# A graph layer's step loop: four selection matrices in place of two, and late coefficients kept in memory

## What is computed

```python
# graph layer; feat = layernorm(x), R = 16 relations, B = 8 bases
w_full = jnp.einsum('rb,bdo->rdo', w_comp, weight)
x_rel  = jnp.einsum('nd,rdo->rno', feat, w_full)
msg    = x_rel[etypes, src] * norm                    # one row of 256 per edge
agg    = jax.ops.segment_sum(msg, dst, num_segments=N)
x      = x + relu(agg + h_bias + feat @ loop_weight)
# then: x = x + moe(layernorm(x)), the two best of 16 experts for each node
```

## Time and profile before

| | us |
|---|---|
| runs, median (lowest to highest) | 3831.26 (3829.78 to 3837.68) |
| the profiled execution | 3843.4 |
| its span, first to last instruction | 3841.7 |
| PE busy | 2433.4 |
| POOL busy | 1874.2 |
| DVE busy | 942.2 |
| ACT busy | 682.4 |

### The profile page before, as it was taken

The page is one execution under the profiler, slowest core; times in us unless marked ns, Lnnn a source line. Parts: engine busy times, 40 slices in busy tenths (PEclk is TensorE's granted clock), DMA queues, the critical chain, the costliest instruction groups (busy, mean ns, idle before and its releaser), DMA issues. The chain is left out here.

```text
span 3841.7 us, 44188 instructions
## 1 busy us (share of the span) xinstructions
PE 2433.4 (63%) x11555; PEld 1907.4 (50%) x11556; DVE 942.2 (25%) x2185; ACT 682.4 (18%) x1839; POOL 1874.2 (49%) x2177
## 2 busy tenths in 40 slices
PE   3544454554655655666666666767767756999976
PEld 1422332433543443454454455555556536888865
DVE  4611111121102112121111111112112246333336
ACT  0510000000011111111111122212222211222234
POOL 0466666566546546555545445345544201444433
PEclk9866676776877877888878877888788878999998
DMA  3442333233223223222222223222222242112135
GB/s 117 146 135 85 88 92 88 75 92 97 73 75 90 78 74 94 77 82 80 78 76 78 78 76 90 66 68 78 83 83 64 52 144 93 63 63 63 61 123 189
DMA packets 144937, 337.27 MB, mean 88 GB/s; under 512 B 36515, under 2 KB 52163, under 8 KB 144740
## 3 DMA queue, kind: packets, MB, share of 16 engines
q0 software_dynamic: 89392, 245.59, 21.9%
q1 hardware_dynamic: 34239, 51.42, 3.9%
q10 hardware_dynamic: 21252, 39.56, 3.0%
HBM read 289.22 MB, written 50.42 MB: 88 GB/s over the span
## 5 line engine op out<-in xcount | busy, mean ns | idle before, releaser
L1176 PE MATMUL psW<-rows,S 128*128 x3920 | 1192.7, 459 | 878.2 <-issue 590.9
L994 POOL DMA_INDIRECT rows<-feat,idx x1568 | 1489.9, 950 | 479.6 <-issue 460.5
L1176 PEld LDWEIGHTS psW<-rows,S 128*128 128x128 f32 x3920 | 850.2, 228 | 1215.1 <-issue 1095.4
L1076 DVE TENSOR_TENSOR S<-psHere,coefS 128x896 f32<-128x896 f32 x280 | 303.8, 1091 | 2227.8 <-PE psW L1176 1244.3
L1235 ACT COPY z<-psW 128x256 f32<-128x256 f32 x392 | 145.6, 371 | 2064.1 <-PE psW L1176 1080.2
L977 POOL COPY idx<-srcT 128x7 int32 (+1 forms) x224 | 43.6, 195 | 783.9 <-PE psW L1176 616.4
L1139 PE MATMUL psG<-wb,zT 128*128 128x256 f32 (+1 forms) x1600 | 357.9, 382 | 0.0
L1139 PEld LDWEIGHTS psG<-wb,zT 128*128 128x128 f32 (+1 forms) x1600 | 304.1, 190 | 47.5 <-issue 1.0
L1126 PE MATMUL psZ<-ident,z 128*128 128x128 f32 x784 | 152.5, 352 | 197.1 <-ACT z L1235 91.2
L1126 PEld LDWEIGHTS psZ<-ident,z 128*128 128x128 f32 x784 | 114.8, 180 | 236.0 <-issue 184.5
L1562 PE MATMUL psH<-xT,w1x 128*128 128x128 f32 x1840 | 228.3, 278 | 0.2 <-DVE w1x L1604 0.2
(11 more groups left out here) (254 smaller groups left out, 1449.6 us busy)
## 6 DMA issues: line engine op xcount, KB each, us to landing
rows<-feat,idx POOLq DMA_INDIRECT x1568
g<-expert_rows SPq DMA_DIRECT2D x24, 512.0 KB, 5.8
w1s<-in_L_ffn_w SPq DMA_DIRECT2D x8, 1024.0 KB, 10.7
w2s<-in_L_ffn_w SPq DMA_DIRECT2D x16, 512.0 KB, 10.9
featT<-fT ACTq DMA_DIRECT2D x25, 256.0 KB, 2.2
fts<-featT ACTq DMA_DIRECT2D x25, 256.0 KB
feat<-yt SPq DMA_DIRECT2D x24, 256.0 KB, 2.2
h<-in_x ACTq DMA_DIRECT2D x24, 256.0 KB
```

The costliest lines, as they stand in the source:

```text
L994: e.indirect_dma_start(rows[:, at * H:(at + 1) * H], None, d.feat, bass.IndirectOffsetOnAxis(ap=idx[:, q * GB + u:q * GB + u + 1], axis=0) ...
L1076: e.tensor_tensor(S[h][:, :].rearrange("p (s b n) -> p s b n", s=U, b=B), both[:, h * U:(h + 1) * U, :].unsqueeze(2).to_broadcast([P, U, B ...
L1176: e.matmul(psW[:, bass.ds(bank[u], H)], S[h][:, u * ZC:(u + 1) * ZC], rows[:, bass.ds(slot[u], H)], start=False, stop=True, skip_group_che ...
```

## The change

- `NS = 4` buffers of S in place of two. A buffer may be written once the turn four before is done. The destinations are still compared for two turns at a time.
- PE's and DVE's loops go over four turns in a pass in place of two, and `CTL_PART` is 80, 60, 68, 72. `tile_product` so stands eight times in a pass of PE's loop.
- The look for an ended tile goes one pair further back (`pairs` has two empty entries ahead of it).
- The additional 7 KB per partition for S, and more, come from `coefS`, which holds 31 of 62 chunks. The coefficients of the later 140 turns are made in four small buffers (`late`), stored by SP to `late_coefs` in memory, and brought back by SP in four loads over coefficients that are used up (`CHUNK`).

The diff, cut to its core:

```diff
+NS = 4
+FIRST = TURNS // 2
+LATE = FIRST * U
+NEAR = -(-LATE // CS)
+CHUNK = [(0, 36, 7), (36, 36, 11), (72, 36, 16), (108, 32, 20)]
-CTL_PART = (78, 62, 70, 70)
+CTL_PART = (80, 60, 68, 72)
...
+        DL = 4
+        late = [sb(f"late{i}", [P, CS * B]) for i in range(DL)]
...
+        def coefs_at(n):
+            return coefS[:, n * GN:(n + 1) * GN] if n < NEAR else late[n % DL][:, :]
...
+            def coefs_out(n):
+                e.wait_ge(s_wg, n + 1)
+                if n < NEAR:
+                    e.dma_start(d.coef[:, 0:(NEAR * CS - LATE) * B], coefS[:, LATE * B:NEAR * CS * B]).then_inc(s_near, 16)
+                else:
+                    e.dma_start(d.coef[:, (n * CS - LATE) * B:((n + 1) * CS - LATE) * B], late[n % DL][:, :]).then_inc(s_lst[n % DL], 16)
+            for n in range(total):
+                for t in tile_at(n):
+                    feat_out(t)
+                if n - 2 >= NEAR - 1:
+                    coefs_out(n - 2)
...
-                e.copy(coefS[:, n * GN:(n + 1) * GN], psC[n % 2][:, 0:GN]).then_inc(s_co, 1)
+                if n >= NEAR + DL:
+                    e.wait_ge(s_lst[n % DL], late_before(n))
+                e.copy(coefs_at(n), psC[n % 2][:, 0:GN]).then_inc(s_co, 1)
...
-        S = [sb(f"S{h}", [P, U * ZC]) for h in range(2)]
+        S = [sb(f"S{h}", [P, U * ZC]) for h in range(NS)]
...
+            for k, (t, n, i1) in enumerate(CHUNK):
+                with e.Fori(i0, i1) as i:
+                    rows_in(i)
+                e.wait_ge(s_S, t + n)
+                c = slice(t * U * B, (t + n) * U * B)
+                e.dma_start(coefS[:, c], d.coef[:, c]).then_inc(s_late[k], 16)
+                i0 = i1
+            with e.Fori(i0, NBLK // RB) as i:
+                rows_in(i)
...
-                    if later(i):
-
-                        e.wait_ge(s_P, s0 - U)
+                    if t0:
+                        e.wait_ge(s_P, (i * NS + (t0 + h0 + h - (NS - 1))) * U)
...
+            four(0, 0, 0)
+            with e.Fori(0, FIRST // NS - 1) as i:
+                four(i, NS, NS)
+            for k, (c0, n, _) in enumerate(CHUNK):
+                e.wait_ge(s_late[k], 16)
+                with e.Fori(0, n // NS) as i:
+                    four(i, FIRST + c0, c0)
...
-                with e.Fori(0, n_turns // 2) as i:
-                    for h in range(2):
-                        e.load(regs, ctl[part_of][:, bass.ds(i * 2 + h, 1), :])
+                with e.Fori(0, n_turns // NS) as i:
+                    for h in range(NS):
+                        e.load(regs, ctl[part_of][:, bass.ds(i * NS + h, 1), :])
```

More of the change, by code:

```diff
@@ L49 @@
 TURNS = STEPS // U
-assert TURNS * U == STEPS and TURNS % 2 == 0
+NS = 4
+assert TURNS * U == STEPS and TURNS % (2 * NS) == 0
 SPAD = -(-STEPS // 512) * 512
@@ L54 @@
 SC = -(-STEPS // CS) * CS
+FIRST = TURNS // 2
+LATE = FIRST * U
+NEAR = -(-LATE // CS)
+CHUNK = [(0, 36, 7), (36, 36, 11), (72, 36, 16), (108, 32, 20)]
+assert sum(n for _, n, _ in CHUNK) == TURNS - FIRST and all(n % NS == 0 for _, n, _ in CHUNK) and FIRST % NS == 0
 ZC = B * WIN
@@ L76 @@
 IB = 2 * (RB // GB)
-CTL_PART = (78, 62, 70, 70)
-assert NBLK % RB == 0 and RB % GB == 0 and RB % QB == 0 and sum(CTL_PART) == TURNS
+CTL_PART = (80, 60, 68, 72)
+assert NBLK % RB == 0 and RB % GB == 0 and RB % QB == 0 and sum(CTL_PART) == TURNS and all(n % NS == 0 for n in CTL_PART)
+assert all(t + n <= 8 * i <= TURNS for t, n, i in CHUNK)
 SLOTS = (N * K + X * (P - 1)) // P
@@ L164, in __init__ @@
         self.feat = dram("feat", (NPAD, H), F32)
+        self.coef = dram("late_coefs", (P, (SC - LATE) * B), F32)
         self.featT = dram("featT", (P, NT2, HC * GN2), F32)
@@ L492, in _ @@
             ch.add(e.memset(one[:, :], 1.0))
-            ch.add(e.memset(pairs[:, 0:1, :], 0))
+            ch.add(e.memset(pairs[:, 0:2, :], 0))
             e.memset(room[:, :], 1).then_inc(s_sti, 1)
@@ L614, in expand @@
         s_fst = [sem(f"fT_st{k}") for k in range(DY)]
+        s_wg, s_near = sem("weighed"), sem("near_st")
+        s_lst = [sem(f"late_st{k}") for k in range(DL)]
         NQ = P // CS
@@ L622, in part, with late_before @@
             return HALF if t == NT2 - 1 else P
+        def coefs_at(n):
+            return coefS[:, n * GN:(n + 1) * GN] if n < NEAR else late[n % DL][:, :]
+        def late_before(n):
+            return 16 * ((n - NEAR) // DL)
         def tile_at(n):
@@ L635, in weigh @@
             def weigh(n):
-                c = coefS[:, n * GN:(n + 1) * GN].rearrange("p (s b) -> p s b", b=B)
+                c = coefs_at(n).rearrange("p (s b) -> p s b", b=B)
                 e.wait_ge(s_co, n + 1)
-                e.tensor_tensor(c, c, wgtS[:, n * CS:(n + 1) * CS].unsqueeze(2).to_broadcast([P, CS, B]), ALU.mult)
+                e.tensor_tensor(c, c, wgtS[:, n * CS:(n + 1) * CS].unsqueeze(2).to_broadcast([P, CS, B]), ALU.mult).then_inc(s_wg, 1)
             for g in range(SG):
@@ L667, in _, with feat_out @@
                 e.dma_start(tables[32 * q:32 * q + 1, 0:n * CTL], d.ctl[t0 * CTL:(t0 + n) * CTL].rearrange("(o n) -> o n", o=1)).then_inc(s_ctl, 16)
-            e.dma_start(pairs[:, 1:TURNS // 2 + 1, :].rearrange("o t c -> o (t c)"), d.pairs.rearrange("(o n) -> o n", o=1)).then_inc(s_ctl, 16)
-            for t in range(NT2):
+            e.dma_start(pairs[:, 2:TURNS // 2 + 2, :].rearrange("o t c -> o (t c)"), d.pairs.rearrange("(o n) -> o n", o=1)).then_inc(s_ctl, 16)
+            def feat_out(t):
                 k, q = t % DY, part(t)
@@ L674, in _ @@
                 e.dma_start(d.feat[t * GN2:t * GN2 + 2 * q, :].rearrange("(p m) f -> p (m f)", m=2), yt[k][0:q, :]).then_inc(s_yst[k], 16)
+            def coefs_out(n):
[4 more added lines that the diff above has]
+                    e.dma_start(d.coef[:, (n * CS - LATE) * B:((n + 1) * CS - LATE) * B], late[n % DL][:, :]).then_inc(s_lst[n % DL], 16)
+            for t in range(EARLY):
+                feat_out(t)
+            for n in range(total):
+                for t in tile_at(n):
+                    feat_out(t)
+                if n - 2 >= NEAR - 1:
+                    coefs_out(n - 2)
+            for n in range(total - 2, total):
+                coefs_out(n)
+            e.wait_ge(s_near, 16)
+            for k in range(DL):
+                e.wait_ge(s_lst[k], 16 * len(range(NEAR + (k - NEAR) % DL, total, DL)))
             e.wait_ge(s_ctl, 16 * (3 + len(CTL_PART)))
@@ L949, in graph_layer @@
         s_pool, s_turn, s_zr, s_node = sem("pool"), sem("pool_turn"), sem("zero"), sem("node")
+        s_late = [sem(f"late{k}") for k in range(len(CHUNK))]
         s_hot, s_S, s_P, s_clear = sem("hot"), sem("steps_ready"), sem("step_done"), sem("cleared")
@@ L964, in _, with rows_in @@
             e.dma_start(gw[:, :, :], a["L0_ffn_gate_w"].rearrange("(c p) e -> p c e", p=P)).then_inc(s_w, 16)
-            with e.Fori(0, NBLK // RB) as i:
+            def rows_in(i):
                 for q in range(RB // QB):
@@ L968, in _ @@
                     e.sem_inc(s_in, QB)
+            i0 = 0
+            for k, (t, n, i1) in enumerate(CHUNK):
[7 more added lines that the diff above has]
+                rows_in(i)
         @blk.gpsimd
@@ L1061, in look, with pair @@
                     nodes(tile1, P)
-            def pair(i):
-                s2 = i * 2 * U
-                if later(i):
-                    e.wait_ge(s_S, 2 * i)
-                e.tensor_tensor(both, dstS[:, bass.ds(s2, 2 * U)].unsqueeze(2).to_broadcast([P, 2 * U, WIN]),
-                                node_h.unsqueeze(1).to_broadcast([P, 2 * U, WIN]), ALU.is_equal).then_inc(s_hot, 1)
+            def pair(i, t0, c0, h0):
+                turn = i * NS + (t0 + h0)
+                if t0 + h0:
+                    e.wait_ge(s_S, turn)
+                e.tensor_tensor(both, dstS[:, bass.ds(turn * U, 2 * U)].unsqueeze(2).to_broadcast([P, 2 * U, WIN]),
+                                node_h.unsqueeze(1).to_broadcast([P, 2 * U, WIN]), ALU.is_equal).then_inc(s_hot, 2)
@@ L1069, in pair @@
                 for h in range(2):
-                    s0 = (2 * i + h) * U
                     if h == 0:
-                        e.wait_ge(s_hot, i + 1)
-                    if later(i):
-                        e.wait_ge(s_P, s0 - U)
-                    e.tensor_tensor(S[h][:, :].rearrange("p (s b n) -> p s b n", s=U, b=B), both[:, h * U:(h + 1) * U, :].unsqueeze(2).to_broadcast([P, U, B, WIN]),
-                                    coefS[:, bass.ds(s0 * B, U * B)].rearrange("p (s b) -> p s b", b=B).unsqueeze(3).to_broadcast([P, U, B, WIN]),
-                                    ALU.mult).then_inc(s_S, 1)
@@ L1079, in pair @@
[L1079 to L1082, removed]
+                        e.wait_ge(s_hot, turn + 2)
+                    if t0:
+                        e.wait_ge(s_P, (i * NS + (t0 + h0 + h - (NS - 1))) * U)
```

(18 more changed lines are left out.)

## The result

| | before, us | after, us |
|---|---|---|
| runs, median (lowest to highest) | 3834.46 (3829.78 to 3837.68, 4 runs) | 4114.52 (4107.1 to 4122.17, 4 runs) |
| the profiled execution | 3843.4 | 4122.17 |
| its span | 3841.7 | 4120.5 |

The ratio is 1.073, 95% interval [1.071, 1.075]: 280 us slower. The forecast was 4003 us (+172).

The account below looks back on a forecast made before the run. TensorE's own instruction queue was taken to set each turn. On the profiled 3843.4 us, -35 - 15 + 219 + 3 = +172 gave 4015, as a median 4003 us; the forecast's range was 3880 to 4250, the whole range 3775 to 4230.

Parts of the forecast that it names:

- The fetch, +219 us: TensorE's doubled loop body is fetched anew in every pass: +219 us, bounds 0 and 602 us.
- The price of a turn, 2.15 us: Extra time of a fetched turn in TensorE's queue: 6.65 us in a first pass against 4.5, +2.15 us.
- GpSimd's cover, 0.73 left: GpSimd sets the pace before 1000 us and covers TensorE's extra there; 2102 of 2890 us remain, 0.73.
- The slow stretches, 0.5 left: Half of TensorE's jumps are disturbed already and count as 0, leaving 140 turns x 2.15 = 301 us.
- 70 x 8.4 = 590: Sign of the fetch: up to 590 instruction packets on q8, spread over 213 to 3100 us.
- S buffers, -35 us: Four S buffers shorten TensorE's waits for S in the graph layer: -35 us, bounds 0 and 209.6 us.
- Loops of four turns, -15 us: 70 back edges of TensorE's loops go: -15 us, at most 23 us.
- Late coefficients: Stores out on SP's queue delay the graph stage: +3 us; loads back in: 0, at most 43 us.
- a first gather later than 216 us: Sign that the step storing late coefficients ahead of the graph layer is wrong.
- The body is not kept: Answers the rival that TensorE's long body stays in its instruction store: -47 us, 3784 us; faster by this, chance 0.27.
- Fetched, but covered: Rival: TensorE's fetches fall in time it was held back anyway and cancel the gain: 3825 to 3840 us, chance 0.08.
- A new wait of SP: Rival: SP holds back row counts or outgoing buffers stall ScalarE: at most 43 + 14 us, near 3870, chance 0.03.

Follow-up runs that it names:

- code4: The kernel before with only TensorE's loops changed to four turns a pass, two S buffers, coefficients kept as before: 3900.96 us beside 3064.51, ratio 1.272.
- once_code4: code4 with the tile product written once per turn in place of twice: 3035.15 us, ratio 0.990 to the kernel before.
- dead34: The kernel before with 34 never-run matmuls behind an added test at each of a pass's four tile tests: 4243.64 us beside 3844.38, ratio 1.106.
- after_again: The whole change measured once more, on a chip where the kernel before is fast: 3900.98 us beside 3066.34, ratio 1.271.
- once4: The whole change with the tile product written once per turn: 3010.2 us, ratio 0.982; on the slow chip 3802.24 us beside 3844.38, ratio 0.991.
- before_again: The kernel before, unchanged, profiled on a chip where it is fast: 3067.47 us.
- dead2: The kernel before with two never-run matmuls behind an added test at each of a pass's four tile tests: 3904.41 us beside 3844.38, ratio 1.017.
- dead48: The kernel before with 48 never-run matmuls behind an added test at each of a pass's four tile tests: 5477.48 us beside 3066.34, ratio 1.786.
- once2: The kernel before, loops of two turns, with the tile product written once per turn in place of twice: 3040.85 us, ratio 0.992.
- coefs2: The whole change with two S buffers and two turns a pass, so late coefficients alone: 3074.91 us beside 3066.34, ratio 1.003.

## Why the prediction was right, and what was off in it

**The fetch, +219 us.** The mechanism held at each sign: packets spread over the whole stage, a median jump of 1246 ns, turns of 6.8 us, and code4, once_code4 and dead34 show it alone. The term was too small. Take from the 280 us what the other parts are worth (below): 280 - 9 + 6 + 9 = 286 us with the buffers' gain as after_again has it, 311 with the gain that they have in once4. The term was 280 x 2.15 x 0.5 x 0.73, and each factor can be set beside a measurement:

- *The price of a turn, 2.15 us, was too low.* It was read from one first pass, whose back edge leads to code just fetched. In a repeated long pass that jump is the dearest of all: (4130 - 208) ns in a pass of four turns is 0.98 us a turn more, 3.13 in all. Where there are no slow stretches, 836 / 280 = 2.99 us was measured over all turns, and 3.9 us over the last 200 (the table above, code4 less before_again), which GpSimd doesn't cover. What part of the 3.9 is the lower granted clock isn't shown.
- *GpSimd's cover, 0.73 left, was right.* In the first 80 turns code4 loses 61 us where the next 60 lose 222: 836 / (280 x 3.9) = 0.77.
- *The slow stretches, 0.5 left, were read wrongly and hid more than that.* The median jump of 207 ns was taken to say that half of the jumps are disturbed. It is 207 in before_again too, where no register instruction is slow, so it is the plain time of the jump:

```profile
L1165 PEldq COMPARE_BRANCH  x560: 68/207/4341, 215.9 to 2322.4; - x187
```

In the trace before 81 of the 560 jumps take more than 300 ns, and 110 of the 280 turns have a slow register instruction. What was left is 286 / 836 = 0.34 to 311 / 836 = 0.37, if the price is the same on both chips. A quarter of the turns takes at most 4.52 us before and 6.99 after, 4.59 in before_again and 7.03 in after_again, which speaks for that.

So a price too low by a factor of 1.8 met a share left of 0.365 where 0.26 to 0.28 was true. The two errors partly cancelled, and that the forecast came as near as it did is in that part luck. The upper bound of 602 us was no bound: 836 is above it.

**What covered it.** I named GpSimd's pace until 1000 us, and it holds: 14 us were lost there. I also named slow stretches, in which the queue "catches up". What the runs show is that the stretches go: 84 of the 560 executions of L1164 took more than 300 ns before, 25 of L1224 after, and in dead34 the fetched loop alone has none. The longest one falls too, from 1399 to 732 ns, but says little: it is 727 in dead2, which fetches nothing more than the kernel before. Where there are no stretches, in after_again, the whole 836 us come through. Why fetching makes them go isn't shown.

**Packets.** I said up to 70 x 8.4 = 590. There are 739: each pass takes some ten, more than the body is long, and nine in dead34 for 6.4 and in dead48 for 7.2. More is read than the body holds.

**S buffers, -35 us.** once4 against once_code4 is -25 with the late coefficients' +9 in it: -34, where the body stays. In the long body code4 and after_again are equal (on two chips whose times of the kernel before are 2 us apart), so -9 there. "PE psW <- DVE S" fell from 209.6 to 120.9 us, which I had named as the sign of this step. It doesn't show it by itself: on the chips without slow stretches these waits are 137.7 us in code4 with two buffers and 137.4 in after_again with four, and they fall with the buffers only where the body is kept (87.4 to 18.0 us, once_code4 to once4).

**Loops of four turns, -15 us.** once_code4 against once2: -5.7 us. At most 23 was right, and three quarters of it was hidden.

**Late coefficients.** Out: +3, and the first gather starts at 217.6 us in place of 215.1, +2.5. By the sign that I gave, a first gather later than 216 us, the step would be wrong. That sign was badly set: +3 from 215.1 is already past it, and I hadn't looked up the 215.1. In: 0; coefs2 has +8.6 for both, of which some 5 behind the stage I had not seen.

**The rivals.** The body is not kept. "Fetched, but covered" failed in the first result: a third came through. A new wait of SP: "PE psW <- SPq" is 130.7 us after and 374.8 in after_again, 319.3 in before_again; in once4 it is what is left when all else is gone, and the kernel is at its fastest. No loss by it is seen.

## What to carry to other kernels

Count the instructions of a loop's body, also of branches that are seldom taken. Between 5.5 and 7.2 packets of 16 KB TensorE's body stopped being kept here, and then each pass fetched it all, at 1.2 to 1.5 us for each jump and 4.1 to 4.2 us for each back edge, at the median. Before a loop is unrolled further, write a rare branch once instead of in every part: here that turned the loss of 280 us into a gain of 42 where the queue is slow, and into one of 54 where it isn't (24 of these come with the single copy alone, once2). To price a fetch, take whole passes with their back edge, and look whether the time that you count as cover is there whenever the kernel runs.

## What the runs showed that I had not expected

- The kernel before takes 3065 us on two chips and 3831 to 3844 us on others. The whole difference lies in the graph layer, and with it come stretches in which register instructions of TensorE's queue take about 700 ns: 463 of more than 300 ns, 333 us in sum, and none in before_again. DVE's and SP's queues have some as well (59 and 23). How the rest of the 776 us follows from them isn't shown. The change is worth +280 us on the one kind and +835 us on the other.
- Stretches of slow register instructions are gone where TensorE's loop is fetched, within one kernel too (dead34).
- Four loops of one length in one kernel can be kept or fetched each for itself (dead34).
- A back edge to code that isn't there costs 4.1 to 4.2 us at the median (after, code4, dead34), about three times a forward jump.
- Where the body is fetched on the chips without slow stretches the granted clock of TensorE is lower as well: a mean of 0.70 in dead48 and 0.84 in code4, against 0.91 in before_again. TensorE's busy time is 208 us longer in code4 and 615 us longer in dead48 than the 2264 us of before_again. What part of the lost time the clock makes was not tried.
